# Twelve shared products dealt out among the last sequences of a one-core decoder layer

## What is computed

```python
x = x + attention(layernorm(x))                       # 16 heads of 8, causal, rotary factors
x = x + cross_attention(ctx, ctx, layernorm(x))       # one head of 128
x = layernorm(x); logits = x @ router_w.T             # 8 experts, top 2
moe = sum over the 2 chosen experts of weight * (silu(x @ w_gate[e]) * (x @ w_up[e])) @ w_down[e]
shared = silu(x @ sw_gate) * (x @ sw_up) @ sw_down    # F = 256 hidden channels
out = x_residual + moe + sigmoid(x @ gate_w.T) * shared
```

## Time and profile before

| | us |
|---|---|
| median of 3 runs (lowest to highest) | 478.93 (478.83 to 479.94) |
| the profiled execution, its own time | 475.0 |
| its span, first to last instruction | 473.1 |

### The profile page before, as it was taken

The page is one execution under the profiler, slowest core; times in us unless marked ns, Lnnn a source line. Parts: engine busy times, 40 slices in busy tenths (PEclk is TensorE's granted clock), DMA queues, the critical chain, the costliest instruction groups (busy, mean ns, idle before and its releaser), DMA issues.

```text
span 473.1 us, 13582 instructions
## 1 busy us (share of the span) xinstructions
PE 427.4 (90%) x4444; PEld 289.8 (61%) x4444; DVE 358.2 (76%) x1232; ACT 293.0 (62%) x951; POOL 203.5 (43%) x247
## 2 busy tenths in 40 slices
PE   4869799999999999999999988769899999999992
PEld 3424455555655655656555555547688888888782
DVE  5474567879889888888797786779577777777595
ACT  1124678887877877878779877463355555555430
POOL 7802012030343262353324235567166666676490
PEclk9999999999999999999999999559999999999998
DMA  7700000101111111011111003512233333232394
GB/s 191 198 24 26 19 19 31 37 10 35 49 29 50 48 48 49 26 54 47 33 47 53 25 28 110 169 51 76 67 100 98 92 93 92 81 104 62 110 318 135
DMA packets 41604, 34.69 MB, mean 73 GB/s; under 512 B 6464, under 2 KB 36432, under 8 KB 41536
## 3 DMA queue, kind: packets, MB, share of 16 engines
q1 hardware_dynamic: 36478, 24.51, 18.4%
q0 software_dynamic: 4320, 8.99, 5.6%
q10 hardware_dynamic: 738, 0.33, 0.3%
HBM read 17.26 MB, written 12.09 MB: 62 GB/s over the span
## 4 chain that ended last, share of the span: by engine, by line
PE 71%; DVE 12%; issue 6%; ACT 4%; POOL 3%; DMA 2%; SPq 1%; DVEq 0%; ACTq 0%; POOLq 0%
PE ps_scores L860 10%; PE ps_scores L678 7%; PE ps_shared L877 7%; PE ps_shared L725 6%; PE ps_scores L707 6%; PE ps_shared L661 3%; PE ps_shared L868 3%; PE ps_scores L703 3%; PE ps_shared L776 3%; ACT probs L955 2%; PE ps_scores L712 2%; POOL xs L593 2%; PE ps_shared L782 2%; PE ps_shared L787 2%; PE ps_scores L852 2%
## 5 line engine op out<-in xcount | busy, mean ns | idle before, releaser
L611 POOL DMA_INDIRECT ys<-ctx_t,xload x71 | 69.1, 974 | 45.2 <-ACT ctx_t L1052 42.7
L955 ACT ACTIVATE probs<-ps_scores 128x512 f32<-128x512 f32 x128 | 69.8, 608 | 17.9 <-PE ps_scores L712 17.9
L599 POOL TENSOR_TENSOR x1b<-x,bias 128x128 f32<-128x128 f32 x32 | 14.4, 451 | 151.0 <-DVE x L1188 151.0
L593 POOL DMA_INDIRECT xs<-xrow,posu x64 | 66.5, 1039 | 26.3 <-issue 13.2
L860 PE MATMUL ps_scores<-wide,xe 128*128 x213 | 66.9, 422 | 0.0
L951 ACT ACTIVATE s_copy<-ps_scores 128x512 f32<-128x512 f32 x64 | 38.4, 604 | 18.7 <-PE ps_scores L685 18.5
L1372 DVE COPY probs<-ps_shared 128x256 f32<-128x256 f32 x71 | 30.2, 425 | 22.8 <-PE ps_shared L868 22.8
L1167 DVE TENSOR_REDUCE negmax<-ps_scores 128x4 f32<-128x512 f32 x64 | 41.1, 684 | 7.4 <-PE ps_scores L685 6.9
L877 PE MATMUL ps_shared<-wd,probs 128*128 x284 | 43.4, 275 | 0.1
L678 PE MATMUL ps_scores<-wide,qk 32*128 32x512 f32 x256 | 38.4, 671 | 3.3 <-ACT probs L955 3.1
L1042 ACT ACTIVATE xe<-ps_scores 128x128 fp32r<-128x128 f32 x71 | 19.7, 278 | 33.8 <-PE ps_scores L852 33.8
(11 more groups left out here) (220 smaller groups left out, 1012.1 us busy)
## 6 DMA issues: line engine op xcount, KB each, us to landing
xload<-xs SPq DMA_DIRECT2D x71, 66.0 KB, 1.9
wide<-qk SPq DMA_DIRECT2D x64, 64.0 KB, 1.9
wide<-ys SPq DMA_DIRECT2D x8, 512.0 KB, 7.4
ctx_t<-in_ctx SPq DMA_DIRECT2D x32, 64.0 KB, 2.0
out_x<-res SPq DMA_DIRECT2D x8, 256.0 KB, 3.4
ys<-ctx_t,xload POOLq DMA_INDIRECT x71, 2.3
wd<-in_L_ffn_w_down SPq DMA_DIRECT2D x8, 128.0 KB, 3.4
xs<-xrow,posu POOLq DMA_INDIRECT x64, 2.4
```

The lines of the kernel that those rows point to most:

```text
L593: pool.indirect_dma_start(out=xs, out_offset=bass.IndirectOffsetOnAxis(ap=posu[:, g % 2, k, u:u + 1], axis=0), in_=xrow[:, g % 2, k, u, :] ...
L611: pool.indirect_dma_start(out=ys, out_offset=bass.IndirectOffsetOnAxis(ap=xload_i[:, i % XL, C + 1:C + 2], axis=0), in_=ybuf[:, i % 4, :], ...
L955: act.activation(probs[:, b % 2, j * HJ:(j + 1) * HJ, :].rearrange("p a t -> p (a t)"), SC[score_bank(("scores_t", b), j)][:], ACT.Exp)\
```

## The change

The 12 products of `gate_up(0)` are no longer issued in a block behind `ranks(7)`. A table `EARLY_GATES` names ten stages on PE (of slots 37 to 40), behind each of which `run` calls `gate_part` once or twice; each call issues the next of the twelve products. The first call carries the waits that `gate_up(0)` had. DVE's subtraction for round 0 moves from its slot 37 to the end of `tall_sums(31)` in slot 33, ahead of `norm_ffn(27)`; `split(0)` on DVE is empty now. ACT's part of round 0 stays where it was. Nothing else moves, and no operation is added or dropped.

```diff
--- before.py
+++ after.py
@@ -138,6 +138,9 @@
     ],
 }
 LATE = {"weights": 1, "split": 2}
+EARLY_GATES = {("attn_out", 31): 1, ("turn_ffn", 28): 1, ("xscores", 30): 1, ("xout", 29): 1, ("turn_ffn", 29): 1, ("xout", 30): 1,
+               ("turn_xprobs", 31): 2, ("turn_ffn", 30): 1, ("xout", 31): 1, ("router", 30): 2}
+assert sum(EARLY_GATES.values()) == 12
 GROUP_STAGES = ("norm_x_stats", "rstd_x", "norm_x", "turn_x", "project", "route", "ranks")
 ENTRIES = [entry for entries in ORDER.values() for entry in entries]
 FIRST_SLOT = -max(ahead for _, ahead, _, _ in ENTRIES)
@@ -424,6 +427,9 @@
 
                 for name, *args in timeline(engine):
                     stages[name](*args)
+                    if engine == "PE":
+                        for _ in range(EARLY_GATES.get((name, *args), 0)):
+                            stages["gate_part"]()
 
         def put_bank(item):
             return filled[FILL[item][0]]
@@ -797,11 +803,6 @@
             def gate_up(g):
                 k = g % 2
                 pe.wait_ge(xb_split, g + 1)
-                if g == 0:
-                    pe.wait_ge(wgs_split, 1)
-                    pe.wait_ge(maxed, NJ * B)
-                    pe.wait_ge(copied, 2 * B)
-                    pe.wait_ge(exped, NJ * B)
                 if g == AHEAD:
                     pe.wait_ge(xe_h, TILES)
                     pe.wait_ge(xe_split, TILES)
@@ -811,6 +812,25 @@
                         for r, (a, m) in enumerate(((wgs_hi, xT_hi), (wgs_hi, xT_lo), (wgs_lo, xT_hi))):
                             mm = pe.matmul(dst[:], a[:, col:col + 128], m[:, k, :], start=(r == 0), stop=(r == 2))
                         mm.then_inc(done, 1)
+
+            parts = [0]
+
+            def gate_part():
+
+                n = parts[0]
+                parts[0] += 1
+                if n == 0:
+                    pe.wait_ge(xb_split, 1)
+                    pe.wait_ge(wgs_split, 1)
+                    pe.wait_ge(maxed, NJ * B)
+                    pe.wait_ge(copied, 2 * B)
+                    pe.wait_ge(exped, NJ * B)
+                f, up, r = n // 6, n // 3 % 2, n % 3
+                dst, col, done = ((PS, 0, gate_done), (PT, FF, up_done))[up]
+                a, m = ((wgs_hi, xT_hi), (wgs_hi, xT_lo), (wgs_lo, xT_hi))[r]
+                mm = pe.matmul(dst[f][:], a[:, col + f * 128:col + (f + 1) * 128], m[:, 0, :], start=(r == 0), stop=(r == 2))
+                if r == 2:
+                    mm.then_inc(done, 1)
 
             def down(g):
                 pe.wait_ge(h_ready, FT * (g + 1))
@@ -831,9 +851,8 @@
             w.run("PE", dict(turn_x=turn_x, project=project, project_v=project_v, scores=scores, turn_max=turn_max, scores_t=scores_t,
                        values=values, tall_sums=tall_sums, turn_y=turn_y, attn_out=attn_out, turn_x2=turn_x2,
                        xproject=xproject, xscores=xscores, turn_xprobs=turn_xprobs, xout=xout, turn_ffn=turn_ffn,
-                       router=router, ranks=ranks))
-
-            gate_up(0)
+                       router=router, ranks=ranks, gate_part=gate_part))
+
             pe.wait_ge(tables, 2)
             w.ge(drained[2], FILLS[2])
             for k in range(2):
@@ -1176,6 +1195,8 @@
                 dve.tensor_tensor(yn[:].rearrange("p (h d) -> p h d", d=HD), heads[:, :, 0:HD],
                                   ysum[:].rearrange("p (h a) -> p h a", a=1).broadcast_to([T, NH, HD]), ALU.mult)\
                     .then_inc(drain, 1)
+                if b == B - 1:
+                    rests(0)
 
             def one(b):
                 return res[:, b, :]
@@ -1315,6 +1336,10 @@
                 dve.tensor_scalar(ek[:, 0:1], ek[:, 0:1], float(E - 1), None, ALU.min).then_inc(tables, 1)
 
             def split(g):
+                if g > 0:
+                    rests(g)
+
+            def rests(g):
                 dve.wait_ge(xb_hi_done, g + 1)
                 w.ge(up_done, FT * (g - 1))
                 dve.tensor_tensor(xT_lo[:, g % 2, :], x3T[:, g * GB * T:(g + 1) * GB * T], xT_hi[:, g % 2, :].bitcast(fp32), ALU.subtract)\
```

## The result

| | median us | lowest to highest | runs |
|---|---|---|---|
| kernel before | 478.83 | 477.69 to 479.94 | 9 |
| changed kernel | 476.06 | 474.74 to 477.32 | 9 |

The ratio is 0.9948, with a 95% interval of 0.993 to 0.9966: 0.5% faster. The forecast was 480.7 us, in a range from 477.3 to 482.7, slower rather than faster. It was wrong in direction, and the measured time lies outside its range. The ratios of all kernels leave out two executions far above the rest, 504.04 us of rests_only (its median is 478.76 without it) and 1318.42 us of the kernel before.

What follows compares the result with a forecast made beforehand. The bound was the chain through the last small stages, routing and scatters to the first tile, then PE. 0 + 0.57 + 0.23 + 1.0 = 1.8 us, giving 476.8 for the profiled execution, 480.7 us for the median; range 477.3 to 482.7.

Steps and rivals of the forecast that it cites:

- Part 1: Block of twelve products leaves its place behind ranks(7); PE would idle until DVE's table instead; gain 0.
- Part 2: DVE's round 0 subtraction moves ahead of norm_ffn(27), into the chain, making xout(28) and all behind later; cost 0.57 us.
- Part 3: Twelve products dealt among PE's small stages at half clock, nearly all fitting into existing waits; cost 0.23 us.
- the dealt products hold the clock: Rival: dealt products fill PE's idle, keeping full clock from 296 to 311; 478.3 us; chance 0.20.
- Part 4: PE enters gate_up(1) at half clock for 4.0 to 6.0 us, delaying mix(2) and the tiles; cost 1.0 us.
- On the DMA side nothing changes: Claim that the last scatter's landing and tile 1's load only shift with the chain; no separate cost.
- the rival that costs more: Late round 1 shifts DVE's subtractions onto another scatter, adding 2.0 us; 482.7 us or more; chance 0.13.
- I carry the difference over unchanged: The 3.9 us by which the median, 478.93, exceeds the profiled execution, 475.0, added to the forecast as it stood.

Runs made afterwards that it cites:

- rests_only: Kernel before with only DVE's subtraction for round 0 moved to the end of tall_sums(31), the block of products kept; 479.26 us, ratio 1.0007.
- rests_behind: Changed kernel with DVE's subtraction for round 0 one stage later, behind norm_ffn(27); 475.82 us, ratio 0.995.
- after_again: Changed kernel, unchanged, run again for a second profile and more runs; 475.88 us, ratio 0.9947.
- after_ref: Changed kernel, unchanged, as reference on a chip where the kernel before takes 478.95 us; 476.68 us, ratio 0.9962.
- warm_block: Changed kernel with twelve additional products, results unused, behind ranks(7) where PE idles; 478.23 us, ratio 0.9985.
- warm_late2: Changed kernel with twelve additional products behind ranks(7) and DVE's expert rests 4 to 7 moved behind mix(1); 475.50 us, ratio 0.9932.
- spare_products: Kernel before with twelve additional products behind the same ten stages, block and late subtraction kept; 477.05 us, ratio 0.9977.
- before_again: Kernel before, unchanged, run again for a second profile; 478.81 us, ratio 1.0011.
- reduce_instead: Kernel before with DVE's subtractions for experts 4 to 7 replaced by equally long maxima over one SBUF input; 474.88 us, ratio 0.9915.
- late_rests_before: Kernel before with DVE's expert rests 4 to 7 moved behind mix(1); 476.82 us, ratio 0.9962.
- warm_late: Changed kernel with twelve additional products behind ranks(7) and expert rests 4 to 7 behind mix(1), on a chip with the kernel before at 503.27; 502.11 us, ratio 0.998.

## Why the prediction was wrong

**Part 1 (the block, gain 0) was right.** PE idles 5.37 us in its place, released by DVE's table.

**Part 2 (the subtraction, cost 0.57) was right where it was measured and did not count.** 6.23 - 5.69 = 0.54 us on the chain (1.0 in rests_only, with its early fall of the clock); rests_behind takes it away and the median stays. In its profile the 0.5 us is lost again in front of the first tile, which waits for DVE.

**Part 3 (products among the stages, cost 0.23) stood at the wrong clock.** The rival to which I gave 0.20, that the dealt products hold the clock, came in for most executions profiled. From `res` of sequence 28 to `ranks(7)` it was 313.57 - 294.58 = 19.0 us and is 312.45 - 295.15 = 17.3: 1.7 us, for the 2.2 that I had counted. I argued that only one product lies ahead of the fall; in fact the first started with the fall, at 296.03. What I left out is that the clock can come back within the stretch: it did at 299.4, after PE had worked on small stages and dealt products without a gap from 295.6. In after_again the clock did not fall until 311 at all; in after_ref it was back at 302.1. Net of part 2 the changed kernel is 0.3 to 1.4 us earlier at `ranks(7)` than the kernel before in these three profiles, and warm_block, the same program up to there, agrees (23.4). warm_late2, also the same up to there, does not: its clock fell at 303.3 and stayed at half, and `ranks(7)` came at 24.8, no earlier than before. So this share varies between executions, as in spare_products.

**Part 4 (cold round 1, cost 1.0) is the step that failed most: it had the delay right and the sign wrong.** From `gate_up(1)` at 318.98 to the rise it was 4.4 us (2.0 in after_again, 5.0 in after_ref; the forecast had 4.0 to 6.0), and `mix(2)`, which starts at 333.31, is 2.1 us later than the 331.24 of warm_block: within the 1.65 to 2.55 of the forecast. The failing sentence is "On the DMA side nothing changes". The late DVE is what keeps the expert rests off the seventh scatter, which took 0.97 in all three profiles of the changed kernel against 3.66 in the typical one of the kernel before. Undoing the cold start costs 2.2 us instead of giving 1.0. I had named the mechanism as the rival that costs more, with "the number of them stays the same", and only in the direction in which a later DVE meets more scatters. It met fewer.

The Trainium skill, page "SBUF — State Buffer", section "Who interferes with whom", says that a tensor_tensor with two SBUF inputs takes only the read interface and so does not hold up descriptor generation; it marks this as inferred. before_again against reduce_instead shows that a series of them does, 3.66 against 0.97 us; the measurement decides.

**The base was wrong: "I carry the difference over unchanged".** The 3.9 us between the profiled execution and the median were not an offset. Between the two profiles of the kernel before, 0.8 us of them lie ahead of the last `values` product, and for these no cause was found. 1.4 lie between there and the first tile product, with the scatter of 3.66 instead of 1.38, and 1.6 behind it, with a second stretch at half clock. The change acts on the last two. In the one execution that I had, the cost of part 4 met a scatter that was already nearly free; there the sum of the gain and the losses is about 0, as the two first profiles show (475.0 and 475.16).

**What is not settled** is the split of the 2.8 us. late_rests_before gives 2.3 for the scatters alone, spare_products 2.0 for the products alone; together that is more than 2.8, so they overlap. The two profiles nearest the medians, before_again and after_again, differ by 1.2 us up to `ranks(7)`, by 0.9 from there to the first tile product and by 0.6 behind it. The last share goes with the second stretch at half clock: from the first tile product to the end it took 138.3 to 138.5 us in the five profiles without that stretch, 139.2 to 139.4 where it lasted 3.4 us (after_again and five others), and 139.9 and 140.1 where it lasted 6.8 (before_again, warm_block). What decides its length is not shown. Each profile is one execution.

## What to carry to other kernels

Compare a profile's own time with the median first: where the difference is larger than the effects that are priced, it is itself an effect to be found, not an offset. When a step delays an engine that is off the path, ask what its work no longer meets as well as what it now meets. Indirect DMAs on the critical path should be kept clear of back-to-back DVE operations with two SBUF inputs; moving four such operations was worth 2.3 us, nearly as much as the whole change with its 2.8.

## What the runs showed of the hardware

- An indirect DMA issued by POOL 0.26 to 0.27 us after the start of a back-to-back series of five two-input DVE subtractions lasted until some 0.85 us behind the end of the series (3.66, 3.65, 3.65 us in before_again, spare_products, warm_block). So did the fifth scatter, issued 0.93 or 0.94 us after the start of the series before it: 2.99 or 3.00 us (3.30 in warm_block, issued at 0.63). Issued 0.14 us after the start it took 1.38 (before, rests_only), 0.42 us after it 1.11 (after_again), and issued 0.57 to 1.07 us ahead of the series 0.96 or 0.97. Beside operations with one SBUF input it took 0.97.
- A rise of the clock needed no long block of products: in the first profile of the changed kernel it came at 299.4 after small stages and dealt products had left PE no gap from 295.6, in after_ref at 302.1.
- The same kernel had the first fall of the clock in this stretch at 296 and at 301.3 in two executions of the kernel before, and at 296, 311.3 and 295.3 in three of the changed kernel.
- The same program took 5% longer on one chip (503.3 against 479 us). In warm_late against warm_late2 18 of 25 us more lay behind the first tile product.
